# Turning the two quantised feed-forward weights: four DMA transposes in place of TensorE transposes and ScalarE copies

## What is computed

```python
def mx_quant(x):            # blocks of 32 along the contraction axis share an exponent
    amax = jnp.max(jnp.abs(xb), axis=-1, keepdims=True)
    scale = jnp.exp2(jnp.floor(jnp.log2(amax)) - (BITS - 2))
    q = jnp.clip(jnp.round(xb / scale), -2.0 ** (BITS - 1), 2.0 ** (BITS - 1) - 1) * scale
    ...
def mx_linear(x, W, b):
    y = jnp.einsum('btk,ok->bto', mx_quant(x), mx_quant(W))
    return bf16_round(y + b)
h = mx_layernorm(x, ln_w, ln_b)
h = mx_linear(h, W1, b1)    # W1: 1024 x 256
h = mx_gelu(h)
h = mx_linear(h, W2, b2)    # W2: 256 x 1024
```

## Time and profile before

| what | value |
| --- | --- |
| time, median of 3 runs | 292.42 us (292.4 to 292.68) |
| the profiled execution's own time | 291.33 us |
| its span, first to last instruction | 289.6 us |
| busy share of PE, DVE, ACT, POOL | 94%, 90%, 76%, 60% |
| share of DMA queue q1 of the 16 DMA engines | 12.5% |
| mean granted TensorE clock | 0.988 |

### The profile page before, as it was taken

The page is one execution under the profiler, slowest core; times in us unless marked ns, Lnnn a source line. Parts: engine busy times, 40 slices in busy tenths (PEclk is TensorE's granted clock), DMA queues, the critical chain, the costliest instruction groups (busy, mean ns, idle before and its releaser), DMA issues.

```text
span 289.6 us, 5338 instructions
## 1 busy us (share of the span) xinstructions
PE 270.8 (94%) x1640; PEld 165.4 (57%) x1640; DVE 261.2 (90%) x682; ACT 220.2 (76%) x378; POOL 174.1 (60%) x253
## 2 busy tenths in 40 slices
PE   8999998999997998999989998999699989997799
PEld 3776755477554764676566756575346444543454
DVE  3799999996999999999999999999986997799982
ACT  5131866479999699979998889889998899875650
POOL 2746380698466787868786878667777353533321
PEclk9999999999999999999999999999869999999999
DMA  7931200002110020022002200210010000100111
GB/s 239 381 125 36 65 3 0 9 6 71 37 43 0 8 71 15 1 67 77 16 1 63 79 9 5 66 44 9 7 36 5 3 0 0 37 3 1 37 38 38
DMA packets 11053, 12.68 MB, mean 44 GB/s; under 512 B 3216, under 2 KB 8336, under 8 KB 10768
## 3 DMA queue, kind: packets, MB, share of 16 engines
q1 hardware_dynamic: 10592, 11.55, 12.5%
q10 hardware_dynamic: 432, 0.79, 0.7%
HBM read 9.84 MB, written 2.10 MB: 41 GB/s over the span
## 4 chain that ended last, share of the span: by engine, by line
PE 44%; DVE 37%; issue 8%; ACT 6%; POOL 3%; DMA 1%; DVEq 0%; POOLq 0%
DVE nm L1323 9%; PE bank L2122 6%; PE bank L2156 6%; PE bank L2169 5%; DVE st L1278 4%; PE bank L2007 3%; PE bank L2235 3%; PE bank L2210 3%; PE bank L2056 2%; PE bank L2082 2%; DVE gq L1424 2%; PE bank L2069 2%; PE bank L2208 2%; ACT g_sb L877 1%; PE bank L2177 1%
## 5 line engine op out<-in xcount | busy, mean ns | idle before, releaser
L1323 DVE TENSOR_REDUCE nm<-bank 128x4 f32<-128x512 f32 x128 | 83.8, 677 | 0.8 <-PE bank L2122 0.6
L857 ACT ACTIVATE p_sb<-bank 128x512 f32<-128x512 f32 x128 | 72.3, 599 | 12.1 <-PE bank L2156 11.6
L2122 PE MATMUL bank<-kbd,xT 96*128 96x512 f32 x128 | 56.0, 468 | 2.6 <-ACT xT L828 1.5
L2156 PE MATMUL bank<-xT,kbd 104*128 104x512 f32 x128 | 53.0, 444 | 5.3 <-DMA xT<-mT 3.2
L555 POOL TENSOR_TENSOR kbd<-k3r,diag_sb 96x512 fp32r<-96x512 f32 x32 | 33.2, 1052 | 12.9 <-PE bank L2156 12.9
L2156 PEld LDWEIGHTS bank<-xT,kbd 104*128 104x128 f32 x128 | 24.6, 193 | 18.6 <-ACT p_sb L857 6.4
L2122 PEld LDWEIGHTS bank<-kbd,xT 96*128 96x128 f32 x128 | 24.4, 193 | 17.9 <-DVE nm L1323 10.8
L2169 PE MATMUL bank<-p_sb,va_sb 128*32 128x512 f32 x256 | 33.3, 610 | 0.0
L509 POOL TENSOR_TENSOR rs<-ve,nhalf 128x2 f32<-128x2 f32 (+1 forms) x36 | 26.1, 725 | 4.6
L504 POOL TENSOR_SCALAR ve<-mv 128x2 f32<-128x2 f32 (+1 forms) x36 | 8.4, 234 | 33.5 <-DVE mv L1284 31.8
L2043 PE MATMUL bank<-wkv_r,xt_r 128*128 128x512 f32 x84 | 23.8, 405 | 0.7 <-DVE r_sb L1301 0.7
(11 more groups left out here) (133 smaller groups left out, 619.1 us busy)
## 6 DMA issues: line engine op xcount, KB each, us to landing
xt_sb<-in_xt SPq DMA_DIRECT2D x8, 256.0 KB, 2.9
x_sb<-in_x SPq DMA_DIRECT2D x8, 256.0 KB, 2.9
out_dram<-o_sb SPq DMA_DIRECT2D x7, 256.0 KB, 2.2
k_sb<-in_ctx SPq DMA_DIRECT2D x8, 192.0 KB, 3.0
x_all<-in_w SPq DMA_DIRECT2D x1, 1024.0 KB, 6.2
w_raw<-in_w SPq DMA_DIRECT2D x1, 1024.0 KB, 8.3
p_sb<-in_wkv ACTq DMA_DIRECT2D x2, 256.0 KB, 3.9
cv_sb<-in_ctxv SPq DMA_DIRECT2D x8, 64.0 KB, 2.0
```

The lines of the kernel that those rows point to most:

```text
L857: sc.activation(p_sb[:, k, :], bankB[k % 2][:, :], ACT.Exp, scale=SCORE_SCALE).then_inc(s_ex, 1)
L1323: ve.tensor_reduce(nm[:, b, u, g, :], bankA[(2 + k + 11 * b) % 2][:, :].rearrange("p (k t) -> p k t", k=KU), AX.X, ALU.max, negate=True).t ...
L2122: mm(bankA[(2 + k + 11 * b) % 2][:, :], xT[0:MR, b, u, g, :], kbd[0:MR, b, u, :, :].rearrange("r k t -> r (k t)"), start=True, stop=True). ...
L2156: mm(bankB[k % 2][:, :], kbd[0:MR + 2 * KU, b, u, kk, :], xT[0:MR + 2 * KU, b, u, :, :].rearrange("r g s -> r (g s)"), start=True, stop=Tr ...
```

## The change

`weights_T` and `weights` are gone from TensorE's and ScalarE's programs, with the semaphores `s_wt` and `s_wcp`. SP gets four `transpose_weight(n, half)`, each a DMA transpose of 128x1024 bf16 (256 KB) from `wqb` in SBUF to half of `w1T` or `w2T` in SBUF, which waits for the two slices `j` that it reads. `w1T` is laid out by output chunk, so that one transpose fills a contiguous half. `h_T(0)` now waits for both halves of `w1T`, and the first `ffn_down` of each sequence of pair 0 for both halves of `w2T`.

```diff
-        w1T = sb("w1T", [P, KC, F], BF16)
+        w1T = sb("w1T", [P, FC, KC, P], BF16)
...
+            def transpose_weight(n, half):
+                for j in (2 * half, 2 * half + 1):
+                    sp.wait_ge(s_wc[n][j], 3)
+                if n == 0:
+                    dst = w1T[:, half * FC // 2:(half + 1) * FC // 2, :, :].rearrange("p j c m -> p (j c) m")
+                else:
+                    dst = w2T[:, :, half * P:(half + 1) * P]
+                sp.dma_start_transpose(dst, wqb[:, n, half * F:(half + 1) * F]).then_inc(s_wtd[n], 16)
...
                 max_rows(1, 0)
+                transpose_weight(0, 0)
+                transpose_weight(0, 1)
                 max_rows(1, 1)
                 load_x(3)
                 load_keys(3)
+                transpose_weight(1, 0)
                 spread_bias()
                 load_xt(4)
+                transpose_weight(1, 1)
                 max_rows(2, 0)
...
-                weights(0)
...
-                weights(1)
...
-                weights(2)
...
-                weights(3)
...
-                        pe.wait_ge(s_wcp, 4)
+                        pe.wait_ge(s_wtd[0], 32)
...
-                    last = mm(bk[:, :], hT[:, c, b, :], w1T[:, c, cols], start=False, stop=c == KC - 1)
+                    last = mm(bk[:, :], hT[:, c, b, :], w1T[:, chunks, c, :], start=False, stop=c == KC - 1)
...
+                if not later(p):
+                    pe.wait_ge(s_wtd[1], 32)
...
-                weights_T(0)
...
-                weights_T(1)
...
-                weights_T(2)
...
-                weights_T(3)
```

More of the change, by code:

```diff
@@ L228, in decoder_kernel @@
         s_wc = [[sem(f"weight{n}_steps{j}") for j in range(4)] for n in range(2)]
-        s_wt = sem("weights_transposed")
-        s_wcp = sem("weights_copied")
+        s_wtd = [sem(f"weight{n}_landed") for n in range(2)]
         s_kvp = sem("kv_projected")
@@ L812, in first_x1_high_again @@
                 sc.activation(x3[:, b, :, :, 1, :], x3[:, b, :, :, 0, :].bitcast(F32), ACT.Copy).then_inc(s_x0c, 1)
[L814 to L822, removed]
             def x1T(p, b, u):
@@ L2205, in ffn_up @@
                     pe.wait_ge(s_y1, 4 * p + n)
-                cols = slice(h * 512, (h + 1) * 512)
+                cols, chunks = slice(h * 512, (h + 1) * 512), slice(h * FC // 2, (h + 1) * FC // 2)
                 bk = ffn_bank(p, b, h)
@@ L2236, in ffn_down @@
                 last.then_inc(s_f2, 1)
[L2238 to L2247, removed]
-                    if n < 2:
-                        src = wqb[:, 0, j * D + n * P:j * D + (n + 1) * P]
-                    else:
-                        src = wqb[:, 1, (n - 2) * F + j * P:(n - 2) * F + (j + 1) * P]
-                    last = tp(dst[:, j, :], src, idb[:, :])
-                last.then_inc(s_wt, 1)
             def head():
```

## The result

| kernel | median | lowest to highest | executions |
| --- | --- | --- | --- |
| before | 292.41 us | 291.23 to 295.3 | 20 |
| the change | 294.34 us | 291.43 to 297.07 | 20 |

The ratio is 1.0053, with a 95% interval from 1.0027 to 1.0079: the change is slower by about 0.5%, 1.5 us. The forecast said slower, but by 8.9%. Three more measurements of the unaltered change, on other chips, gave 1.0066, 1.0045 and 1.0088. Ratios here leave out the disturbed, slow executions (two of the change's twenty, and later one of 329 us and one of 1,419 us among them), so they can differ from the quotient of the medians, which is 1.0066 in this table.

The account below looks back on a forecast made before the run. TensorE (94% busy) and VectorE (90%) were taken to bound the kernel, with `hq` gating `h_T(0)`. Waits of 14.8 and 8.1 plus 3.0 for the clock, 25.9 us, gave 317.2, as median 318.3 us; range 292 to 335.

Parts of the forecast that it names:

- What bounds the kernel, and what the removal is worth: At `h_T(0)`, gated by VectorE's `hq`: removing 2.08 us of TensorE's transposes gains 0 to 0.3 us.
- The length T of one transpose: Each DMA transpose of 256 KB on SP's queue: taken as 9.7 us, with ends of 1.1 and 82 us.
- the lower end: Shortest bound on one transpose, from the trace's price for 256-byte packets: 1.1 us.
- 14.8 us at the maxima rows: TensorE waits at `scores_b(1, 1, 0)` for `max_rows(1, 1)`, queued behind both W1 transposes and landing at 85.6 us.
- 8.1 us at the bias product: TensorE waits for the copies of `spread_bias`, queued behind the third transpose and landing at about 97.7 us.
- T = 2.9: Case in the range by transpose length: 2.2 us lost, about 294.6 us in all.
- `load_xt(4)` "has room": On SP's queue behind the third transpose: this load, read by TensorE from 84.05 us, would not come late.
- The clock: TensorE's granted clock falls after the second stall: 3.0 us charged, including 1.4 us for `max_rows(2, 0)`.
- as fast as plain copies: Rival for the transposes: each below 2.3 us, no DMA late, 292.2 us, same; chance 0.18.
- Only partly late: Rival for TensorE's stalls: transposes of 2.3 to 7 us, same two stalls but smaller, 293 to 309 us; chance 0.20.
- The forecast's sign, slower: Whole kernel slower than before, by stalls of TensorE behind the queued transposes: chance 0.75.

Follow-up runs that it names:

- e3: The change with no transposes of either sort, the turned weights being constants that GpSimd writes at the start: ratio to before 0.9986.
- e4: The kernel before, turning one of eight blocks in each round of weight transposes, ScalarE's copies kept in full: ratio to before 0.9987.
- e16: The unaltered change, measured again on one chip with three load-order variants: 294.24 us, ratio to before 1.0088.
- e5: The unaltered change, measured again: ratio to before 1.0066.
- e7: The change with its four DMA transposes replaced by plain DMA copies of the same 256 KB, weights left unturned: ratio to before 1.0011.
- e13: The change with the bias loads and load_xt(4) issued ahead of both W2 transposes: 292.46 us, ratio to before 1.0013.
- e6: The change with six dummy products in TensorE's wait near 89 us: ratio to before 1.0047.
- e1: The change with TensorE's removed work put back as dummies, eight small products at each of the four old places: ratio to before 1.0009.
- e2: The kernel before, its own transposes kept, with four DMA transposes into unread memory added at the change's places: ratio to before 1.0022.
- e8: The kernel before with six dummy products near 89 us and ten more near 203 to 208 us: ratio to before 1.0086.
- e10: The change with one more dummy product at the start and TensorE's removed work put back as dummies: ratio to before 1.0010.
- e15: The kernel before with four DMA transposes into unread memory, load_xt(4) issued behind all four: 294.07 us, ratio to before 1.0087.
- e11: The change with its four transposes issued from ScalarE's DMA queue, where its old copies stood: ratio to before 1.0008.
- e9: The change with one more dummy product at the start of TensorE's program: ratio to before 1.0086.
- e12: The unaltered change, measured once more: ratio to before 1.0045.
- e14: The change with load_xt(4) issued behind the fourth DMA transpose as well: 293.53 us, ratio to before 1.0062.

## Why the prediction was wrong

- **What bounds the kernel, and what the removal is worth:** right. `hq` gates `h_T(0)`; TensorE now waits 0.76 us for it, the removed 2.08 us buy nothing, and e3 and e4 put the whole removal at 0.9986 and 0.9987, with 1 inside both intervals.
- **The length T of one transpose:** this step failed. I chose pieces of 32 B at 19 ns, 9.7 us. Measured were about 1,056 packets of 249 B, 1.4 us, close to the lower end, which the prediction had worked out as 1.1 us from the earlier trace rows for 256-byte packets. The error was the choice of the middle between ends that lay a factor of 75 apart, although the rows nearest in size said 1.1. Both terms that rest on it, 14.8 us at the maxima rows and 8.1 us at the bias product, fall away. The maxima rows are late by 0 to 0.8 us (0.47 in e16), hidden by the wait for `hq` but for 0.2 us in e5, and the bias copies not at all. Two smaller slips change nothing: the small copy's data move in three slices, 0.45 us, not 0.6, and by the prediction's own terms T = 2.9 gives 1.2 + 1.3 = 2.5 us, not 2.2.
- **Two rules of the Trainium skill that disagreed:** the rule of "Advanced Engine Details and Errata", section "X-Bar Transpose (TRN2)", was the nearer one: an estimated 0.7 us against 1.4 measured, at 156 to 212 GB/s in place of the 350 to 400 stated. Its other sentence, that transposes are as fast as regular DMAs, doesn't hold here either: e7's plain copies moved at up to 379 GB/s, 0.8 us each. The 1309 ns per 128x128 block from "VectorE: DVE Perf Modes", section "The three transpose paths", don't scale: here eight blocks together took 1.4 us to move.
- **`load_xt(4)` "has room":** the second step that failed, and the one on which the real loss hangs. I looked for the first reader of `xt_sb` on TensorE, at 84.05 us. The first reader is GpSimd, at 74.64, which already waited 2.36 us for this load and had 1.70 us of room behind it. Issued 1.5 to 2.2 us later, and landing 0.2 to 0.6 us more slowly (3.14 us from issue to use in e16, 3.56 in e5, 2.95 before), the load used this up: in e16 `xt_r` starts 2.36 us later than before, and `kbd` 0.61 us. What it costs is best told by e16 against e13, 1.78 us by the medians.
- **The clock:** 3.0 us were charged after stalls that didn't come. A stretch near 91 us does appear in some profiles and costs 1.0 to 1.2 us, but filling the idle time there bought nothing in e6, whose ratio stayed at 1.0047, and e3 has the stretch without a loss in the median.
- **The rivals:** the branch "as fast as plain copies" described the transfers best, since no DMA that the prediction followed was late enough to cost. Its time, 292.2 us, missed the 1.5 us of GpSimd and VectorE. "Only partly late" has the right sign and size, 293 to 309 us, but by T from 2.3 to 7 and stalls of TensorE for the maxima and the bias, which the traces don't show in that size: that it fits the time is luck. No rival had this mechanism. The forecast's sign, slower, was luck too, since neither of the two stalls that it was added up from came.

What stays open: what sets the issue time of `k_sb`, and what decides whether the clock falls near 91 us. The issue of `k_sb` took 0.45 to 0.75 us in the six profiles of kernels with all of TensorE's work (before, e1, e2, e8, e10, e15), and 0.66 to 1.66 us in the twelve without it (e4 keeps an eighth). e3 and e4 are among these, and they issue no DMA transpose. The relief of TensorE may therefore make the load late in the change's order, by way of this issue: that would explain why e1 and e10, with an x of 15.70 and 15.72, lose nothing. It is an agreement of profiles, and no run tests it. No run here beats the kernel before. The nearest versions with DMA transposes are e11 (1.0008) and e13 (1.0013), which can't be told from it.

## What to carry to other kernels

When a DMA is added to an in-order queue, list every transfer behind it and ask for each which engine touches it first, on all engines, and what wait stands right behind that reader: the room is that wait, not the distance to TensorE's use. GpSimd's waits for a busier engine can be worth keeping, since they held its work in step with VectorE's here: an engine that was off the critical path became costly by moving 0.4 to 0.7 us later (e9, e16, e12), and in e8 by moving earlier. And where a cost is unknown by a factor of 75, weigh the ends by the rows that are nearest in size before taking the middle.

## What the runs showed of the hardware

- A DMA transpose of 128x1024 bf16 from SBUF to SBUF holds the issuing engine for 1.23 to 1.39 us, but for one of 2.10 us in e1 and one of 1.94 in e10 (a plain copy of the same 256 KB 0.53 to 0.68, e7). It moves in 1.4 us where the plain copy takes 0.8, and lands 3.1 to 5.4 us after its issue (the plain copy 2.3 to 3.5).
- VectorE's CAST of 128x32 lasted 0.24 to 0.99 us, depending on when GpSimd's addition started; in the 16 profiles in which GpSimd was first it ended 1.36 to 1.38 us after that start, and in the two in which VectorE was first (e14, e15) it lasted 0.24.
- The mean granted clock and the time don't go together: e8's profiled execution had the highest of all profiles, 0.994, at 293.29 us against 291.33.
- A higher clock of TensorE can cost time through another engine: in e8 GpSimd's `kbd`, freed earlier, lay beside VectorE's `gq`, which took 1.42 us in place of 0.68.
